# Attention passes: destination scores as float32r halves in one product, and work tables of 16-bit numbers

## The chip, the core and the metric

The kernel runs on one NeuronCore of a Trainium2 chip. The metric is the device time of one execution in microseconds. TensorE multiplies, VectorE (DVE), ScalarE (ACT) and GpSimd (POOL) do the rest, SyncE (SP) issues most DMAs and GpSimd the gathers. In the profile PE is TensorE's product and PEld its weight load; a name with q behind it (DVEq, ACTq, PEldq) is the sequencer of that engine, which loads registers, branches and waits.

## The reference

Four graph layers run one behind another on 3125 nodes with 256 features and 103125 edges, sorted by destination. Each starts with `h = relu(layernorm(x))` and adds its result to `x`: a typed attention layer (L0), a weighted sum over edges (L1), an edge MLP with a gate (L2), and a graph attention of two convolutions (L3). The change touches the two convolutions in earnest:

```python
h = (x @ W).reshape(N, HEADS, HEAD_DIM)            # 8 heads of 32
alpha_s = jnp.einsum('nhc,hc->nh', h, a_src)
alpha_d = jnp.einsum('nhc,hc->nh', h, a_dst)
e = alpha_s[src] + alpha_d[dst]
e = jnp.where(e > 0, e, NEG_SLOPE * e)
m = jax.ops.segment_max(e, dst, num_segments=N)
ex = jnp.exp(e - m[dst])
denom = jax.ops.segment_sum(ex, dst, num_segments=N)
alpha = ex / (denom[dst] + 1e-16)
out = jax.ops.segment_sum(h[src] * alpha[:, :, None], dst, num_segments=N)
```

## The kernel before

**Tiling.** Edges are taken in supertiles of 1024 (128 partitions x 8 slots); there are 102. Nodes lie in 25 blocks of 128. Since edges are sorted by destination, a supertile's destinations fall into one block, and into a second one for 24 of the 102 supertiles. What must be known of this is worked out on the chip by `prepare()` (lines 364 to 374) into two small tables on partition 0, `work` (line 163, blocks of 128 nodes) and `typed_work` (line 171, windows of 104 nodes for the typed pass). Row `s + 1` has four 32-bit numbers for supertile `s`: the numbers of the first extra block and of the one behind the last, the first block, and how many extra ones there are. An engine that needs them loads the row into registers: `work_of` (line 699) and `work_typed` (line 796).

**The passes.** In order: the typed pass (`typed_pass`), the weighted pass, the edge MLP pass, and then twice, for the layers of the graph attention: `gat_tables` (line 1979), `gat_pass` (line 2064) and `gat_normalise`. `gat_tables` computes, block by block, `h @ W` and the two scores of each node and head; it writes `h` with the source scores as rows of 264 numbers to a table in HBM and keeps the destination scores in `dst_alpha`, 25 x 8 numbers per partition (reduction at line 2044).

**One attention pass.** Three supertiles make a group (34 groups), two groups a turn of the hardware loop. Of a group with number q:

- GpSimd gathers the source rows (line 731), 8 gathers of 128 rows for each supertile, into one of six slots. A slot is free when the messages of the supertile five before the awaited count are made.
- SyncE loads destination numbers as rows (`dst_row`) and penalties for the scans.
- ACT makes of a row of destination numbers a one-hot matrix `hotrow` (lines 2285 and 2286: square of the difference to the node number, then relu(1 - square)), and `xhotrow` for an extra block.
- TensorE brings each edge the score of its destination (`expand`, `bring`, line 2370): for each of the 8 slots the one-hot matrix is the weight operand (128x128, float32) and the block's 8 destination scores are the moving one; the extra block is added into the same place of `psE`.
- VectorE adds the source scores from the gathered rows (line 2164) and takes the leaky relu (line 2166); TensorE turns the scores (line 2406), VectorE scans for the running maxima (lines 2244 and 2245), TensorE turns them back (line 2414).
- VectorE subtracts (`diff`, line 2253), ACT takes the exponential (line 2337), VectorE makes the messages (line 2233), and TensorE sums them by destination with a one-hot matrix (`scatter`, line 2385), and once more for an extra block. VectorE merges the sum into the node's values with the running maximum (`combine`, lines 2175 to 2186).

The order is written out by hand in the functions `group` of each engine. On TensorE a group is: scatter(0), the turned scores of the next group, scatter(1), scatter(2), the turning back for the next group, and then the three brings of the group after next:

```python
                        scatter(s + 2, 2, g % 2)
                        if next_scores:
                            turn_back(q + 1)
                        scatter_extra(s + 2, g % 2)
                        if next_rows:
                            for u in range(U):
                                expand(q + 2, u)
```

The next product in line is scatter(0) of the next group. On VectorE a group is: diff, messages(0), the scores of the next group, messages(1), combine(0), messages(2), the scans of the next group, combine(1), combine(2). A bring's product before the change:

```python
last = nc.tensor.matmul(group_view(psE)[:, j, u, :], onehots[:, j, :],
                        dst_alpha[:, ds(b, 1), :].squeeze(1), start=(fresh and j == 0),
                        stop=True, skip_group_check=True)
```

Of the kernel before, what the change touches and what calls it, by code (L numbers as in the profile page):

```python
# [19 lines left out]
F32 = mybir.dt.float32  # L20
BF16 = mybir.dt.bfloat16
I32 = mybir.dt.int32
ALU = mybir.AluOpType
# [3 lines left out]
P = 128  # L27
D = 256
SLOTS = 8
# [4 lines left out]
H3 = 8  # L34
DE = 64
U = 3
# [17 lines left out]
def ds(i, n):  # L54
    return bass.ds(i, n)
# [23 lines left out]
def gnn(nc, a, out, n_nodes, n_edges):  # L79
# [83 lines left out]
    work = sb(top, "work", [1, NS + 2 * U + 2, 4], I32)  # L163
# [7 lines left out]
    typed_work = sb(early, "typed_work", [1, NS + 2 * U + 2, 4], I32)  # L171
# [1807 lines left out]
    def gat_tables(layer, dst_alpha, elu_source):  # L1979


        with Stage(("h", "low", "low_exp", "elu", "hT_ps", "hT", "y", "rows", "alphas", "link_dve"), ("w_in", "r_out")) as st:
# [11 lines left out]
            with nc.Block() as block:  # L1994
# [28 lines left out]
                def _(dve):  # L2023
# [11 lines left out]
                    with dve.Fori(0, NB) as b:  # L2035
# [11 lines left out]
                        dve.wait_ge(S["alphas"], START + b + 1)  # L2047

# [15 lines left out]
    def gat_pass(layer, dst_alpha):  # L2064
# [6 lines left out]
        with Stage(("idx_staged", "scored", "hotrow", "expanded", "x_hotrow", "x_expanded", "to_scan_ps",  # L2071
# [8 lines left out]
            hotrow = st.sb("hotrow", [P, U, SLOTS, P])  # L2080
            xhotrow = st.sb("xhotrow", [P, SLOTS, P])
# [23 lines left out]
            lanes = psX[0:LANES, :]  # L2105

# [3 lines left out]
            with nc.Block() as block:  # L2110
# [42 lines left out]
                def _(dve):  # L2153
# [3 lines left out]
                    def edge_scores(i, g):  # L2157
                        q = 2 * i + g
                        for u in range(U):
                            slot_rows_in(dve, U * g + u, i)  # L2160
                        _, x1, _, _ = work_of(dve, U * q + U)
                        dve.wait_ge(S["expanded"], START + U * q + U)
                        dve.wait_ge(S["x_expanded"], START + x1)
                        link(v.tensor_tensor(et[:, :, :, :], group_view(psE),
                                             rows[:, U * g:U * g + U, :, D:GAT_W].rearrange("p u j h -> p j u h"), ALU.add))
                        v.scalar_tensor_tensor(et[:, :, :, :], et[:, :, :, :], 0.2, et[:, :, :, :], ALU.mult,
                                               ALU.max).then_inc(S["scored"], 1)
# [195 lines left out]
                def _(pe):  # L2363
                    def expand(q, u):
# [3 lines left out]
                        def bring(onehots, b, fresh):  # L2368
                            for j in range(SLOTS):
                                last = nc.tensor.matmul(group_view(psE)[:, j, u, :], onehots[:, j, :],  # L2370
                                                        dst_alpha[:, ds(b, 1), :].squeeze(1), start=(fresh and j == 0),
# [109 lines left out]
    with top:  # L2481
# [11 lines left out]
        dst_alpha = sb(top, "dst_alpha", [P, NB, H3])  # L2493
        weight = sb(middle, "weight", [P, NT + U * SLOTS])
# [13 lines left out]
        for layer in (1, 2):  # L2508
            gat_tables(layer, dst_alpha, layer == 2)
            gat_pass(layer, dst_alpha)  # L2510
# [52 lines left out]
```

## Time and profile before

| | |
|---|---|
| median of 3 runs | 8833.31 us |
| lowest, highest | 8825.69, 8842.84 us |
| span of the profiled execution | 8830.1 us |
| TensorE busy (products) | 6600.0 us, 75% |
| VectorE busy | 5164.4 us, 58% |
| GpSimd busy | 4060.3 us, 46% |
| ScalarE busy | 2234.7 us, 25% |
| mean granted TensorE clock | 0.819 of full speed |

The profiled execution is not one of the three timed ones. Its own time is known as its span, from the first to the last instruction, 8830.1 us, which is 3.2 us below the median. The span has five long stretches: the typed pass (about 600 to 2115 us), the weighted pass (2555 to 3690), the edge MLP pass (3860 to 5920) and the two attention passes (6095 to 7380 and 7505 to 8790). Between them lie short stages over the nodes. An engine that is busy for most of a stretch sets its length; where none is, the length comes from waits between the engines, which the timeline shows one by one.

### The profile page before, as it was taken

The page shows a single profiled execution, that of the slowest core. Times are in us where ns is not written, and L with a number is a line of the kernel's source. Part 1 is how long each engine was busy: PE and PEld are TensorE (multiplying, and loading weights), DVE is VectorE, ACT ScalarE, POOL GpSimd, SP SyncE. Part 2 cuts the span into 40 slices and gives each one's busy share as a digit, 9 for nine tenths or more (in the row PEclk, how much of TensorE's full clock was granted, in tenths as well). Part 3 has the DMA queues.
Part 4 walks back from the last instruction along what each step waited for, and adds up shares of the span by engine and source line. Part 5 has one row for each costly group of instructions (what it writes and reads, how often), then busy time and mean ns, then how long its engine had stood idle before and what let it go on. Part 6 is the DMA issues. An engine that isn't in the chain of part 4 may idle for free. (4 is left out here: it accounts for less than half of the span.)

```text
span 8830.1 us, 116392 instructions
## 1 busy us (share of the span) xinstructions
PE 6600.0 (75%) x27378; PEld 5018.6 (57%) x27379; DVE 5164.4 (58%) x9644; ACT 2234.7 (25%) x4857; POOL 4060.3 (46%) x4373
## 2 busy tenths in 40 slices
PE   4977777774736666679999999974788885787886
PEld 2546566563525444546666666653676673666665
DVE  3138888886243333246666666665666666566666
ACT  1222222221310000123333333332333331333332
POOL 0025555552037777124444444423666661666663
PEclk9988888886857777589999999986777776677777
DMA  2247767666013333133343344332444441544443
GB/s 92 99 144 212 214 208 213 207 209 151 4 57 105 105 105 105 29 108 115 115 124 114 116 121 116 117 83 85 135 139 135 131 140 37 149 133 135 136 135 90
DMA packets 440058, 1096.42 MB, mean 124 GB/s; under 512 B 102452, under 2 KB 177296, under 8 KB 439410
## 3 DMA queue, kind: packets, MB, share of 16 engines
q0 software_dynamic: 249344, 763.23, 30.9%
q1 hardware_dynamic: 190180, 328.60, 11.1%
q14 instruction: 507, 4.15, 0.2%
q8 instruction: 27, 0.44, 0.0%
HBM read 1009.55 MB, written 81.94 MB: 124 GB/s over the span
## 5 line engine op out<-in xcount | busy, mean ns | idle before, releaser
L731 POOL DMA_INDIRECT st_rows<-g_table,st_stage_idx x1632 | 1558.0, 955 | 873.4 <-issue 463.6
L824 POOL DMA_INDIRECT st_rows<-kv_table,st_stage_idx x832 | 806.2, 969 | 671.1 <-PE st_psM L1167 391.2
L2385 PE MATMUL st_psM<-st_msg,st_hot 128*128 128x273 f32 x3264 | 942.6, 449 | 128.0 <-DVE st_msg L2233 102.6
L677 POOL DMA_INDIRECT st_rows<-p_table,st_stage_idx x816 | 854.3, 1047 | 302.9 <-issue 220.3
L731 POOL DMA_INDIRECT st_rows<-h_table,st_stage_idx x816 | 777.0, 952 | 244.5 <-issue 234.8
L2385 PEld LDWEIGHTS st_psM<-st_msg,st_hot 128*128 128x128 f32 x3264 | 702.9, 221 | 321.5 <-DVE st_msg L2233 91.2
L1519 DVE TENSOR_TENSOR st_pre<-st_psP,st_rows 128x512 f32<-128x512 f32 x816 | 523.5, 682 | 531.5 <-PE st_psP L1610 392.6
L1616 PE MATMUL st_psC<-st_w,st_rT 128*128 128x256 f32 x3264 | 814.7, 392 | 0.0
L1616 PEld LDWEIGHTS st_psC<-st_w,st_rT 128*128 128x128 f32 x3264 | 587.3, 190 | 373.7 <-ACT st_rT L1577 212.3
L1426 PE MATMUL st_psM<-st_rows,st_hot 128*128 128x256 f32 x1632 | 512.3, 484 | 372.5 <-DMA st_rows<-h_table,st_stage_idx 190.4
L1426 PEld LDWEIGHTS st_psM<-st_rows,st_hot 128*128 128x128 f32 x1632 | 401.3, 251 | 480.7 <-issue 331.3
L1572 ACT ACTIVATE st_gate<-st_pre 128x256 f32<-128x256 f32 x816 | 340.4, 417 | 1276.2 <-DVE st_pre L1519 1276.2
L2370 PE MATMUL st_psE<-dst_alpha,st_hotrow 128*128 x3264 | 589.7, 323 | 66.5 <-issue 34.2
L2370 PEld LDWEIGHTS st_psE<-dst_alpha,st_hotrow 128*128 128x128 f32 x3264 | 585.6, 281 | 72.8 <-issue 70.8
L1149 PE MATMUL st_psE<-st_q_rows,st_hotrow 104*128 104x256 f32 x1664 | 513.5, 477 | 39.6 <-ACT st_hotrow L1076 18.5
L673 POOL COPY st_stage_idx<-src_idx 128x8 int32 x102 | 19.3, 189 | 1117.1 <-DVE st_pre L1519 850.5
L2233 DVE TENSOR_TENSOR st_msg<-st_rows,st_psU 128x2048 f32<-128x2048 f32 x204 | 465.4, 2281 | 111.1 <-ACT st_psU L2337 111.1
L1610 PE MATMUL st_psP<-st_wb,st_eaT 64*128 64x512 f32 x1632 | 461.6, 642 | 53.4 <-DVE st_pre L1519 47.8
L1149 PEld LDWEIGHTS st_psE<-st_q_rows,st_hotrow 104*128 104x128 f32 x1664 | 404.0, 249 | 128.7 <-issue 33.9
L1167 PE MATMUL st_psM<-st_rows,st_hot 128*128 128x262 f32 x1632 | 376.7, 389 | 51.3 <-DVE st_rows L1035 51.1
L2385 PE MATMUL st_psZ<-st_msg,st_xhot 128*128 128x273 f32 x768 | 253.9, 498 | 202.9 <-DVE st_xhot L715 202.9
L1361 DVE TENSOR_TENSOR node_values<-node_values,st_psM 128x256 f32 x228 | 94.8, 416 | 510.1 <-PE st_psM L1426 385.3
(394 smaller groups left out, 11250.1 us busy)
## 6 DMA issues: line engine op xcount, KB each, us to landing
st_dst_row<-in_dst_row SPq DMA_DIRECT2D x310, 512.0 KB, 5.7
kv_table<-st_rows_out SPq DMA_DIRECT2D x25, 1560.0 KB, 5.7
st_ea<-in_ea SPq DMA_DIRECT2D x103, 256.0 KB, 3.8
st_rows<-g_table,st_stage_idx POOLq DMA_INDIRECT x1632, 2.8
st_pens<-pen_table SPq DMA_DIRECT2D x208, 72.0 KB
st_rows<-kv_table,st_stage_idx POOLq DMA_INDIRECT x832, 4.5
st_rows<-h_table,st_stage_idx POOLq DMA_INDIRECT x816, 2.7
st_rows<-p_table,st_stage_idx POOLq DMA_INDIRECT x816, 3.7
```

The costliest lines, as they stand in the source:

```text
L677: pool.indirect_dma_start(out=rows[:, u * SLOTS + j, :], out_offset=None, in_=table, in_offset=bass.IndirectOffsetOnAxis(ap=stage_idx[:, u ...
L731: pool.indirect_dma_start(out=rows[:, slot, j, :], out_offset=None, in_=table, in_offset=bass.IndirectOffsetOnAxis(ap=stage_idx[:, g, u * ...
L824: pool.indirect_dma_start(out=rows[:, slot, j, :], out_offset=None, in_=kv_table, in_offset=bass.IndirectOffsetOnAxis(ap=stage_idx[:, g, u ...
L1149: last = nc.tensor.matmul(psE[h][:, j * D:(j + 1) * D], onehots[0:NQ, h * HALF + j, :], queries, start=(fresh and j % 2 == 0), stop=True, ...
L1167: last = nc.tensor.matmul(out[:, 0:SUM_W], onehots[:, j, :], rows[:, slot, j, D:D + SUM_W], start=(j == 0), stop=(j == SLOTS - 1))
L1426: last = nc.tensor.matmul(out[:, 0:D], onehots[:, j, :], rows[:, slot, j, :], start=(j == 0), stop=(j == SLOTS - 1))
L1519: v.tensor_tensor(pre[:, j % DEEP, :], psP[y][:, :], rows[:, u * SLOTS + j, :], ALU.add).then_inc(S["pre"], 1)
L1610: nc.tensor.matmul(psP[y][:, :], eaT[lo:lo + DE, u, k, :], wb[lo:lo + DE, :], start=True, stop=True).then_inc(S["pre_ps"], 1)
L1616: last = nc.tensor.matmul(psC[y][:, 0:D], rT[:, (2 * k + y) % DEEP, c, :], w2[:, c, :], start=(c == 0), stop=(c == 1))
L2233: v.tensor_tensor(msg[:, n, :, 0:GAT_W].rearrange("p j (h c) -> p j h c", h=H3)[:, :, :, 0:HW3 - 1], rows[:, slot, :, 0:D].rearrange("p j ...
L2370: last = nc.tensor.matmul(group_view(psE)[:, j, u, :], onehots[:, j, :], dst_alpha[:, ds(b, 1), :].squeeze(1), start=(fresh and j == 0), s ...
L2385: last = nc.tensor.matmul(out[:, 0:MSG_W], onehots[:, j, :], msg[:, n, j, :], start=(j == 0), stop=(j == SLOTS - 1))
```

## The change

The destination scores are kept a second time as `dst_split`, in float32r, a float32 with a shortened mantissa: a high half (the score converted) and a low half (what the conversion left off). The one-hot matrices are float32r too. One product per slot brings both halves, 16 columns instead of 8, into `psE`; VectorE adds the high halves to the source scores and then the low ones. The two work tables hold unsigned 16-bit numbers instead of 32-bit ones; the functions that read them are unchanged.

```diff
-    work = sb(top, "work", [1, NS + 2 * U + 2, 4], I32)
+    work = sb(top, "work", [1, NS + 2 * U + 2, 4], U16)
...
-    typed_work = sb(early, "typed_work", [1, NS + 2 * U + 2, 4], I32)
+    typed_work = sb(early, "typed_work", [1, NS + 2 * U + 2, 4], U16)
...
-    def gat_tables(layer, dst_alpha, elu_source):
+    def gat_tables(layer, dst_alpha, dst_split, elu_source):
...
                         last.then_inc(S["alphas"], 1)
                         dve.wait_ge(S["alphas"], START + b + 1)
+                    link.turn()
+                    link(v.tensor_copy(dst_split[:, :, 0, :], dst_alpha[:, :, :]))
+                    link(v.tensor_tensor(dst_split[:, :, 1, :], dst_alpha[:, :, :], dst_split[:, :, 0, :].bitcast(F32), ALU.subtract))
...
-            hotrow = st.sb("hotrow", [P, U, SLOTS, P])
-            xhotrow = st.sb("xhotrow", [P, SLOTS, P])
+            hotrow = st.sb("hotrow", [P, U, SLOTS, P], F32R)
+            xhotrow = st.sb("xhotrow", [P, SLOTS, P], F32R)
...
+            def split_view(n):
+                return psE[:, 0:SLOTS * U * 2 * H3].rearrange("p (j u n h) -> p j u n h", j=SLOTS, u=U, n=2)[:, :, :, n, :]
+
...
-                        link(v.tensor_tensor(et[:, :, :, :], group_view(psE),
+                        link(v.tensor_tensor(et[:, :, :, :], split_view(0),
                                              rows[:, U * g:U * g + U, :, D:GAT_W].rearrange("p u j h -> p j u h"), ALU.add))
+                        link(v.tensor_tensor(et[:, :, :, :], split_view(1), et[:, :, :, :], ALU.add))
...
-                                last = nc.tensor.matmul(group_view(psE)[:, j, u, :], onehots[:, j, :],
-                                                        dst_alpha[:, ds(b, 1), :].squeeze(1), start=(fresh and j == 0),
+                                at = (j * U + u) * 2 * H3
+                                last = nc.tensor.matmul(psE[:, at:at + 2 * H3], onehots[:, j, :],
+                                                        dst_split[:, ds(b, 1), :, :].rearrange("p b n h -> p (b n h)"), start=(fresh and j == 0),
                                                         stop=True, skip_group_check=True)
...
+        dst_split = sb(top, "dst_split", [P, NB, 2, H3], F32R)
```

## Rows read from the trace of the kernel before

**Rows 1.** Busy time by stretch: us, PE, PEld, DVE, ACT, POOL, PEclk, DMA share, GB/s

```profile
600.00:2115.00 1515.00, 1098.48 (x4322) 902.33 (x4321) 1310.61 (x1772) 351.19 (x483) 812.06 (x880) 0.81 0.70 209
2555.00:3690.00 1135.00, 713.97 (x2230) 558.20 (x2230) 362.79 (x1244) 22.09 (x48) 785.04 (x851) 0.74 0.34 95
3860.00:5920.00 2060.00, 1919.67 (x8956) 1346.93 (x8956) 1353.23 (x2831) 713.47 (x1842) 868.76 (x913) 0.98 0.40 117
6095.00:7380.00 1285.00, 1017.18 (x4576) 861.62 (x4576) 793.42 (x1310) 415.13 (x918) 785.14 (x848) 0.75 0.45 131
```

**Rows 2.** Costliest groups: xcount | busy us, mean ns | idle before them, releasers

```profile
L731 POOL DMA_INDIRECT st_rows<-g_table,st_stage_idx x1632 | 1558.0, 955 | 873.4 <-issue 463.6
...
L2385 PE MATMUL st_psM<-st_msg,st_hot 128*128 128x273 f32 x3264 | 942.6, 449 | 128.0 <-DVE st_msg L2233 102.6
...
L2370 PE MATMUL st_psE<-dst_alpha,st_hotrow 128*128 x3264 | 589.7, 323 | 66.5 <-issue 34.2
...
L2370 PE MATMUL st_psE<-dst_alpha,st_xhotrow 128*128 x768 | 169.8, 359 | 74.0 <-ACT st_xhotrow L2286 73.7 <-issue 0.2
```

**Rows 3.** Waits from 6095 to 8790 us: us in total, times, longest

```profile
POOL st_rows L731 <- DVE st_msg L2233: 400.4, 95, 12.2
...
DVE st_et L2164 <- DMA st_rows<-g_table,st_stage_idx: 173.0, 19, 22.5
...
DVE st_et L2164 <- PE st_psE L2370: 133.0, 32, 7.8
...
PE st_psE L2370 <- ACT st_xhotrow L2286: 73.7, 27, 3.1
```

**Rows 4.** Timeline of TensorE, four groups: start us, us, merged instructions, idle before

```profile
6465.13 10.18 PE L2370 MATMUL st_psE<-dst_alpha,st_hotrow 128*128 x48 [1.12 <-issue]
...
6478.57 5.85 PE L2385 MATMUL st_psM<-st_msg,st_hot 128*128 128x273 f32 x16
...
6505.89 6.90 PE L2370 MATMUL st_psE<-dst_alpha,st_hotrow 128*128 x48
6515.89 5.98 PE L2385 MATMUL st_psM<-st_msg,st_hot 128*128 128x273 f32 x16 [3.10 <-DVE st_msg L2233]
...
6548.03 3.58 PE L2370 MATMUL st_psE<-dst_alpha,st_xhotrow 128*128 x16 [1.88 <-ACT st_xhotrow L2286]
6551.46 3.56 PE L2370 MATMUL st_psE<-dst_alpha,st_hotrow 128*128 x16
6554.87 6.94 PE L2385 MATMUL st_psM<-st_msg,st_hot 128*128 128x273 f32 x16
...
6587.78 5.87 PE L2385 MATMUL st_psM<-st_msg,st_hot 128*128 128x273 f32 x16 [1.45 <-DVE st_msg L2233]
```

**Rows 5.** Timeline of VectorE in the same groups

```profile
6472.64 2.29 DVE L2233 TENSOR_TENSOR st_msg<-st_rows,st_psU 128x2048 f32<-128x2048 f32 x1 [2.07 <-ACT st_psU L2337]
6480.09 0.36 DVE L2164 TENSOR_TENSOR st_et<-st_psE,st_rows 128x192 f32<-128x192 f32 x1 [5.16 <-DMA st_rows<-g_table,st_stage_idx]
...
6484.46 0.16 DVE L2175 TENSOR_SCALAR st_absent<-st_psM 128x1 f32<-128x1 f32 x1 [1.29 <-PE st_psM L2385]
...
6548.11 2.29 DVE L2233 TENSOR_TENSOR st_msg<-st_rows,st_psU 128x2048 f32<-128x2048 f32 x1 [2.02 <-ACT st_psU L2337]
6555.15 0.36 DVE L2164 TENSOR_TENSOR st_et<-st_psE,st_rows 128x192 f32<-128x192 f32 x1 [4.75 <-PE st_psE L2370]
```

**Rows 6.** Two lines of TensorE, weight loads: duration ns min/median/max, first and last start

```profile
L1616 PEld LDWEIGHTS st_psC<-st_w,st_rT x3264: 186/190/337, 3875.7 to 5913.4; 128*128 128x128 f32 x192
...
L1624 PEld LDWEIGHTS st_psR<-ident,st_pre x1632: 139/140/144, 3878.5 to 5914.1; 128*128 128x128 f32 x182
```

**Rows 7.** VectorE's loads in the typed pass (line 797), and idle time before `hot` there

```profile
L797 DVEq TENSOR_LOAD <-typed_work x308: 337/344/754, 592.9 to 2106.4; - x154
...
DVE st_hot L715 <- issue: 98.0, 51, 2.4
```

**Rows 8.** The leaky relu at line 2166: duration ns min/median/max

```profile
L2166 DVE SCALAR_TENSOR_TENSOR st_et<-st_et x68: 357/358/407, 6125.4 to 8742.8; 128x192 f32<-128x192 f32 x68
```

More of the change, by code:

```diff
@@ L20 @@
 F32 = mybir.dt.float32
+F32R = mybir.dt.float32r
 BF16 = mybir.dt.bfloat16
 I32 = mybir.dt.int32
+U16 = mybir.dt.uint16
 ALU = mybir.AluOpType
@@ L2062, in _, with gat_pass @@
                         last.then_inc(S["y"], 1)
-    def gat_pass(layer, dst_alpha):
+    def gat_pass(layer, dst_split):
         with Stage(("idx_staged", "scored", "hotrow", "expanded", "x_hotrow", "x_expanded", "to_scan_ps",
@@ L2508, in gnn @@
         for layer in (1, 2):
-            gat_tables(layer, dst_alpha, layer == 2)
-            gat_pass(layer, dst_alpha)
+            gat_tables(layer, dst_alpha, dst_split, layer == 2)
+            gat_pass(layer, dst_split)
             group_passes[0] += 1
```

## The prediction

> **What bounds the kernel now.** I read the passes one by one first. In the typed pass VectorE is busy 1310.6 of 1515 us, in the weighted pass GpSimd issues gathers all the time, in the edge MLP pass TensorE is busy 1919.7 of 2060 us at a clock of 0.98 [rows 1]. The work tables are read in all of them. The reader should see that only the two attention passes (1285 us each) have no engine near its limit: TensorE 1017 us, VectorE 793 us, GpSimd 785 us plus its issue gaps. They are bound by a ring of waits.
>
> The ring, per group of three supertiles: TensorE turns the scanned maxima back, brings the destination scores of the group after next (line 2370), and only then can start scatter(0), the first of the group's three message sums (line 2385). VectorE in that time makes `diff` and the first messages, and then waits for psE and the gathered rows (line 2164). GpSimd needs 24 x (955 + 300) ns = 30.1 us for a group's gathers [rows 2]; two groups of the timeline take 6548.11 - 6472.64 = 75.5 us, 37.7 each [rows 5]. So the gathers are not the bound: GpSimd waited 400.4 us for messages to free its slots [rows 3].
>
> **The change, part by part. First the size of the product.** A bring is eight products. Today each is two records (204 brings, 3264 records; 48 extra ones, 768), 589.7 + 169.8 = 759.5 us busy [rows 2]. Sixteen records take 3.58 us at the low clock, 0.22 us each; three brings that began at the high one took 6.90 us, 0.144 each [rows 4]. The moving side is only 8 columns, so the pace is that of the weight loads. A float32 load takes 190 ns and a load for a transpose, which is one record per product over the same 128 columns, 140 ns [rows 6]; latency included, that is one pass of columns less. I take a float32r product as one record with a one-pass load: half the records, half the time of each, a bring of 0.9 us instead of 3.58. The 16 moving columns stay under the load. Upper end: half the records at the old pace, 1.8 us. Lower end: 8 x 0.06, 0.5 us. TensorE sheds 570 us by the middle value, 380 by the upper end.
>
> **What of that is on the path.** I follow four groups in the timelines [rows 4, 5].
> - Group one: the brings ran until scatter(0) began at 6478.57, though its messages were done at 6474.93. But VectorE then stood until 6480.09 for gathered rows, not for psE. What is won is its later wait for scatter(0), 1.3 us.
> - Group two: scatter(0) at 6515.89 had waited 3.10 us for messages. The three brings were covered. Won: 0.
> - Group three: TensorE waited for ACT's extra one-hot until 6548.03, then ran two brings to 6555.0. With 0.9 us each they end at 6549.8, ahead of the messages (6550.40). VectorE's 4.75 us wait for psE goes, scatter(0) starts at 6550.5 instead of 6554.87: 4.4 us won.
> - Group four: scatter(0) waited 1.45 us for messages. Won: 0.
>
> That is 5.7 us in four groups; the pattern of extra blocks repeats about so, and there are 68 groups: 17 x 5.7 = 97 us. The other count is the total of VectorE's waits for psE, 133.0 us in 32 groups [rows 3]. Four groups are a small sample, so I take the middle of the two, 115 us. Lower end 54: bring of 1.8 us, group three wins 3.2, group one nothing. Upper end 133 + 17 x 1.3 = 155.
> What is late next, where the brings go: the messages themselves (groups two and four), ACT's extra one-hot row (TensorE waited 73.7 us for it [rows 3], and still will), and gathered rows (173.0 us [rows 3]).
>
> **The added operation.** VectorE adds the low halves: one more 128x192 operation per group, 358 ns [rows 8], 0.39 us start to start with its link, ahead of `scored`, for which the turned scores on TensorE wait. In groups two to four VectorE stands after it for scatter(0) anyway, so it is covered there; behind it in group one are messages(1) and GpSimd's slot. 17 x 0.39 = +7 us; without cover 68 x 0.39 = +27.
> **Tables.** Two more operations over 200 elements after the loop of each layer, 4 x 0.39 = 1.5 us, while the last rows of the table are on their way to HBM: I cost them at 0 to 1.5, take 1. ACT writes the one-hot rows as float32r, same count and shape: 0; the bound, 5% of 1148 ns, would be hidden while ACT, busy 415 of 1285 us [rows 1], stands idle, except ahead of the extra bring.
>
> **The work tables.** Each read of a table row is already one load of four numbers; on VectorE it takes 344 ns [rows 7]. Narrower numbers leave the count of loads alone. The trace has no load of another width. One end: it becomes as cheap as a register operation, near 60 ns, -0.28 each; other end: narrow reads cost as much more, +0.28. Exposed are those ahead of which VectorE has nothing queued: in the typed pass the idle time before `hot` is 98.0 us in 51 groups [rows 7], 1.9 us each, two loads of it, and one more ahead of the scores: 3 x 51 = 153. In the attention passes, with the engines waiting on one another, I count 1.5 per group, 100. In the weighted and the MLP pass GpSimd and TensorE cover them. Half the bytes may save a little and are unlikely to save most: I take -0.06, 250 x -0.06 = -15 us; ends -70 and +70.
> The Trainium skill (DMA: Bandwidth & Descriptors, "Latency and other measured facts") gives `tensor_load` a floor of about 600 ns. The trace does not agree (344 ns). If there is a floor all the same, at this trace's own value, then the width saves nothing and the sum would be 15 us less.
>
> **The sum.** -115 + 7 + 1 - 15 = -122 us against the profiled span of 8830.1 us: 8708. The median of the runs is 8833.3, 3 us above that execution, so 8711, and I say 8710. What a measurement of this kernel can tell from no change is 0.2%, 18 us.
>
> **The rivals.**
> - *More than that.* VectorE's waits for psE all go, waits for scatter(0) with them, and the loads really get short: 155 + 70 = 225 less, 8605. For it: the 400.4 us that GpSimd stands waiting, so nothing stops it until a group takes 30.1 us. Against: groups two and four win nothing. Chance 0.17, from 8570 to 8640.
> - *Mostly hidden.* The bring stays at 1.8 us, the messages, the extra one-hot and the gathered rows take over, the added operation is on the path everywhere: -54 + 27 + 0 = -27, 8806. For it: two of four groups. Chance 0.14, 8770 to 8815.
> - *It does not do what it says.* A float32r product with so few moving columns is still run as two records with two-pass loads. Then nothing is saved and 7 to 27 us are added: 8840 to 8860, or with cheaper loads no change. Chance 0.07.
> - *Slower: the clock.* The sums are priced by TensorE's clock. 204 of them take 942.6 us, 4.62 each [rows 2]; one that began at the low level took 6.94 [rows 4]. With the brings short, TensorE stands idle for longer ahead of each sum, and more of them could begin or stay at 1.2 GHz. If the mean rises half-way to 6.94, to 5.8: 204 x 1.2 = +240 us, less the 122: 8950. It decides from a rise of 0.6 us per sum (122/204). Against: scatter(0) begins at the low level today as well (5.85, 5.98, 6.94 and 5.87 us in the four groups [rows 4]), because the brings do not keep the clock up, so there is little left to lose. Chance 0.07.
> The Trainium skill (TensorE: Matmul & The Clock Gate, "What's actually happening") says that throttled is the default and activity releases it. By that rule a TensorE with less work is the slower one per product, and this rival would come in; the trace agrees that idle stretches and small products go with the low clock, and speaks for no loss only by the four rows just named.
>
> **How the numbers follow.** Likeliest, 0.55: the ring loosens by what the brings delayed, 8640 to 8770, told as 8710. The range reaches over it and most of its two neighbours, from 8600 (both upper ends) to 8800 (lower end of the product, little from the loads). Outside are the clock, no effect and the tails. Faster by over 0.2%: 0.55 + 0.17 + 0.14 = 0.86; within 0.2%: most of the third rival, 0.05; slower: the clock and the rest, 0.09.
>
> **What the profile of the changed kernel would show.** At line 2370 (shifted) 1632 + 384 records instead of 3264 + 768, busy under 250 us, loads near 140 ns at the high clock. VectorE's wait for psE at the first score addition under 30 us instead of 133.0. GpSimd's wait for messages down by about 100 from 400.4. Scatter(0) directly behind its messages in all groups without an extra block, mean of the sums still 4.4 to 4.9 us. TENSOR_LOAD on VectorE between 0.25 and 0.344 us, and the typed pass shorter by up to 10 us; the weighted and the MLP pass unchanged. It is wrong if the records do not halve (third rival), if sums get longer than 5.2 us (fourth), or if the waits for gathered rows and for ACT's one-hot grow by what the brings gave up (second).

## The result and the profile after

The change makes the kernel slower. In paired runs before took 8832.07 us (median of 4) and after 9124.14 us (9118.15 to 9131.29): ratio 1.0332, 95% interval 1.0319 to 1.0345, 292 us more. The profiled execution of after has a span of 9128.0 us, 297.9 more than that of before.

Where the time came in is read first, by the first and the last gather of each pass. Kernel before, the gathers of one table each (duration ns min/median/max, first to last start):

```profile
L824 POOL DMA_INDIRECT st_rows<-kv_table,st_stage_idx x832: 941/947/1745, 593.7 to 2079.8; - x167
...
L731 POOL DMA_INDIRECT st_rows<-h_table,st_stage_idx x816: 942/947/1067, 2558.1 to 3585.7; - x164
...
L677 POOL DMA_INDIRECT st_rows<-p_table,st_stage_idx x816: 942/947/1912, 3854.2 to 5879.2; - x164
...
L731 POOL DMA_INDIRECT st_rows<-g_table,st_stage_idx x1632: 940/947/1198, 6092.7 to 8727.7; - x182
```

Kernel after, the same rows:

```profile
L826 POOL DMA_INDIRECT st_rows<-kv_table,st_stage_idx x832: 940/946/1917, 604.9 to 2255.3; - x167
...
L733 POOL DMA_INDIRECT st_rows<-h_table,st_stage_idx x816: 942/946/1066, 2732.8 to 3758.6; - x164
...
L679 POOL DMA_INDIRECT st_rows<-p_table,st_stage_idx x816: 941/947/1912, 4025.6 to 6109.6; - x164
...
L733 POOL DMA_INDIRECT st_rows<-g_table,st_stage_idx x1632: 940/946/1218, 6323.8 to 9031.1; - x182
```

The typed pass is 164 us longer (1650.4 against 1486.1), the weighted pass nearly the same (1025.8, 1027.6), the edge MLP pass 59 us longer (2084.0, 2025.0), the attention passes 72 (2707.3, 2635.0). The three that grew account for 295 of the 297.9 us. The float32r product is in the attention passes alone, so in the typed and the edge MLP pass only the tables can be at work. The loads of the tables in after (against VectorE's 344 ns in [rows 7]):

```profile
L799 DVEq TENSOR_LOAD <-typed_work x308: 941/949/1615, 604.1 to 2280.8; - x154
...
L703 PEldq TENSOR_LOAD <-work x612: 981/987/1009, 2731.9 to 9080.9; - x153
L703 ACTq TENSOR_LOAD <-work x612: 879/887/937, 6322.7 to 9081.7; - x153
...
L703 DVEq TENSOR_LOAD <-work x476: 942/948/970, 2740.0 to 9083.5; - x159
```

A load of four 16-bit numbers takes 949 ns on VectorE, 0.60 us more than one of four 32-bit numbers. Their count is the same (308). VectorE's idle time ahead of its work in the typed pass shows it; after, with before's row for `hot` in [rows 7] (98.0 us in 51) and before's other row at line 950 below it:

```profile
DVE st_hot L717 <- issue: 234.8, 101, 4.6
DVE st_rows L952 <- issue: 63.9, 51, 1.3
```

```profile
DVE st_rows L950 <- issue: 33.0, 51, 0.7
```

"Issue" is time in which the engine waited for nothing that the profile shows but its own sequencer: 136.8 + 30.9 = 168 us more, about the typed pass's 164. The product itself did what it says; TensorE's groups in the attention passes of after, answering to [rows 2]:

```profile
L2395 PE MATMUL st_psM<-st_msg,st_hot 128*128 128x273 f32 x3264 | 953.0, 453 | 284.5 <-DVE st_msg L2242 183.4 <-issue 101.0
L2380 PE MATMUL st_psE<-dst_split,st_hotrow 128*128 x1632 | 320.3, 330 | 129.1 <-issue 96.0 <-ACT st_hotrow L2295 33.1
...
L2380 PE MATMUL st_psE<-dst_split,st_xhotrow 128*128 x384 | 89.8, 363 | 185.7 <-ACT st_xhotrow L2295 185.7
```

The records have halved (1632 + 384) and the busy time with them, 759.5 to 410.1 us (320.3 + 89.8). But each still takes 330 ns, as before (323).

### The profile page after: what moved, and what is told of

It reads as the page before. It is cut to its first block and busy times, and to the rows that moved or that the text cites. A ratio compares the mean times of both kernels' runs of the same rounds, so it can differ in the third digit from the quotient of the medians.

```text
span 9128.0 us, 112436 instructions
## 1 busy us (share of the span) xinstructions
PE 6326.0 (69%) x25362; PEld 4709.1 (52%) x25363; DVE 5189.8 (57%) x9716; ACT 2255.5 (25%) x4857; POOL 4075.6 (45%) x4373
## 5 line engine op out<-in xcount | busy, mean ns | idle before, releaser
L733 POOL DMA_INDIRECT st_rows<-g_table,st_stage_idx x1632 | 1561.3, 957 | 950.0 <-DVE st_msg L2242 476.4
L2395 PE MATMUL st_psM<-st_msg,st_hot 128*128 128x273 f32 x3264 | 953.0, 453 | 284.5 <-DVE st_msg L2242 183.4
L1618 PEld LDWEIGHTS st_psC<-st_w,st_rT 128*128 128x128 f32 x3264 | 587.2, 190 | 373.7 <-ACT st_rT L1579 212.3
L1428 PEld LDWEIGHTS st_psM<-st_rows,st_hot 128*128 128x128 f32 x1632 | 393.1, 246 | 483.7 <-issue 328.2
L1151 PE MATMUL st_psE<-st_q_rows,st_hotrow 104*128 104x256 f32 x1664 | 551.0, 504 | 85.0 <-issue 60.9
L1151 PEld LDWEIGHTS st_psE<-st_q_rows,st_hotrow 104*128 104x128 f32 x1664 | 430.2, 265 | 185.5 <-issue 79.1
L2380 PE MATMUL st_psE<-dst_split,st_hotrow 128*128 x1632 | 320.3, 330 | 129.1 <-issue 96.0
L1169 PEld LDWEIGHTS st_psM<-st_rows,st_hot 128*128 128x128 f32 x1632 | 315.1, 196 | 151.7 <-issue 100.4
L2380 PEld LDWEIGHTS st_psE<-dst_split,st_hotrow 128*128 128x128 f32 x1632 | 309.7, 287 | 139.0 <-issue 137.1
```

What stands on the lines that cost most here:

```text
L733: pool.indirect_dma_start(out=rows[:, slot, j, :], out_offset=None, in_=table, in_offset=bass.IndirectOffsetOnAxis(ap=stage_idx[:, g, u * ...
L1151: last = nc.tensor.matmul(psE[h][:, j * D:(j + 1) * D], onehots[0:NQ, h * HALF + j, :], queries, start=(fresh and j % 2 == 0), stop=True, ...
L1169: last = nc.tensor.matmul(out[:, 0:SUM_W], onehots[:, j, :], rows[:, slot, j, D:D + SUM_W], start=(j == 0), stop=(j == SLOTS - 1))
L1428: last = nc.tensor.matmul(out[:, 0:D], onehots[:, j, :], rows[:, slot, j, :], start=(j == 0), stop=(j == SLOTS - 1))
L1618: last = nc.tensor.matmul(psC[y][:, 0:D], rT[:, (2 * k + y) % DEEP, c, :], w2[:, c, :], start=(c == 0), stop=(c == 1))
L2380: last = nc.tensor.matmul(psE[:, at:at + 2 * H3], onehots[:, j, :], dst_split[:, ds(b, 1), :, :].rearrange("p b n h -> p (b n h)"), start= ...
```

## The experiments

Times are compared by their ratio to the kernel before, run beside each group of experiments on the same chip: its median was 8831.20 us beside e1 to e4, 8828.58 beside e9 to e12 and 8837.26 beside e13 to e16. e5 to e8 ran on a chip on which the kernel before itself takes 10409.62 us. Every variant with a 32-bit table also masks the two loaded numbers that waits are made against. e1 is the kernel before with the mask and one more operation on a semaphore in the typed pass's stores by SyncE (`hold(sp, held)`, in all of these variants), and they are read against it; e3, with no 32-bit table, has no mask and is read against the kernel before. Pass lengths and waits come from one profiled execution of each kernel.

**e1: the mask.**

```diff
+    def masked(eng, values, top):
+        x0, x1, low, more = values
+        x0, x1 = (nc.s_assert_within(eng.snap(x & 0xFFFF), 0, top, skip_runtime_bounds_check_because=BOUNDED) for x in (x0, x1))
+        return x0, x1, low, more
...
-        return values
+        return masked(eng, values, NS * NB)
```

> The kernel before with 32-bit tables, whose two waited-on numbers are also cut to 16 bits in registers (two or so register operations of about 40 ns per load): the base for the float32r part alone. Both theories: loads 340 ns on VectorE as before, 8832 plus 15 to 45 us, so 8850 to 8880.

Measured: 8818.12 us, ratio 0.9986 (0.9976 to 0.9995), not the 8850 to 8880 that I had expected.

**e2: the product alone**, the changed kernel with `I32` in both tables, and the mask.

> The same base plus the whole float32r part, tables of 32 bits. Theory A (the 16-bit loads cost all of the loss and the float32r part gains as in the ring of waits): 100 to 140 us below the base of this call, so about 8740; periods of the attention groups near 35.3 us, VectorE's wait for psE almost gone. Theory B (the shorter products lower the clock or lengthen the sums, and share in the loss): not below the base, 8860 to 8950, mean of the sums over 4.8 us.

Measured: 8782.53 us, 0.9947 (0.9931 to 0.9964). The product gains, as theory A has it, but 36 us against e1 and not 100 to 140.

**e3: the tables alone**, the kernel before with `U16` in both.

> The kernel before with both tables of 16-bit numbers and nothing else. Theory A: loads about 949 ns on VectorE as in the changed kernel; typed pass +164 us, MLP pass +59 us, attention passes +160 us, together 9215. Theory B: the attention passes lose much less by the loads, 9060 to 9120.

Measured: 9168.05 us, 1.0386 (1.0369 to 1.0403); typed pass 1647.7 us, as in after. It lies between the two theories: the typed pass is 162 us longer than before and the edge MLP pass 55, as expected, and the attention passes 110, not 160. So the loss is the tables', +337 us against before, and the product takes some 44 us off it (9168.05 - 9124.14, of two pairs of runs).

**e4: what a load costs.** A stage of loads of each kind, twice, from tiles in SBUF, is added after `prepare`; its own time is not of interest.

```diff
+                    use(dve, [load(w32[0:1, 0:4], engines=[dve.engine], **KW) for _ in range(2)])
+                    use(dve, [load(w32[0:1, 1:5], engines=[dve.engine], **KW) for _ in range(2)])
+                    use(dve, [load(w16[0:1, 0:1], engines=[dve.engine], **KW) for _ in range(2)])
```

> The 16-bit kernel with a small stage behind the preparation in which VectorE and TensorE load 1, 2, 3 or 4 numbers of 32, 16 or 8 bits. Theory A1 (each narrow number is a read of its own, four 32-bit ones are one): 32 bits 1 to 4 numbers all 340 ns on VectorE; 16 bits about 340 for one number and 200 more for each further one: 340, 545, 745, 949. Theory A2 (narrow reads are slow as such, or each load of several takes a slower route): 16 bits near 949 ns whatever the number.

VectorE's loads: L2510 to L2514 are 2, 3, 4, 4 from the second element on, and 8 of 32 bits; L2515 to L2518 are 1, 2, 3 and 4 of 16 bits; L2519 is 4 of 8 bits:

```profile
L2510 DVEq TENSOR_LOAD <-st_w x2: 523/528/532, 84.0 to 84.6; - x2
...
L2511 DVEq TENSOR_LOAD <-st_w x2: 743/748/753, 85.7 to 86.4; - x2
...
L2512 DVEq TENSOR_LOAD <-st_w x2: 348/353/358, 87.7 to 88.1; - x2
...
L2513 DVEq TENSOR_LOAD <-st_w x2: 961/963/965, 89.1 to 90.1; - x2
...
L2514 DVEq TENSOR_LOAD <-st_w x2: 597/598/599, 91.7 to 92.4; - x2
...
L2515 DVEq TENSOR_LOAD <-st_w x2: 289/292/295, 93.7 to 94.1; - x2
...
L2516 DVEq TENSOR_LOAD <-st_w x2: 503/508/513, 94.7 to 95.3; - x2
...
L2517 DVEq TENSOR_LOAD <-st_w x2: 722/724/725, 96.3 to 97.1; - x2
...
L2518 DVEq TENSOR_LOAD <-st_w x2: 941/946/952, 98.3 to 99.3; - x2
...
L2519 DVEq TENSOR_LOAD <-st_w x2: 961/964/968, 101.3 to 102.3; - x2
```

One 16-bit number takes 292 ns and each further one some 218 (292, 508, 724, 946); two and three of 32 bits (528, 748) and four of 8 bits (964) take about as much as that many of 16 bits. Four of 32 bits from the start of the tile are the exception: 353 ns, less than two (528), and eight take 598. The same four from the next element on take 963. So theory A1 holds for the 16-bit numbers and for four of 32 bits; it was wrong for two and three of 32 bits, which it had at 340. The times fit one read of 16 bytes in place of four. That what counts is a start on a 16-byte boundary is inferred: the start of the tile and a start 4 bytes behind it were tried, 8 bytes were not.

**e9: is it the width or the single read?** 32-bit tables, four bytes off the boundary.

```diff
-    work = sb(top, "work", [1, NS + 2 * U + 2, 4], I32)
+    work = sb(top, "work", [1, 4 * (NS + 2 * U + 2) + 4], I32)[:, 1:4 * (NS + 2 * U + 2) + 1].rearrange("p (n k) -> p n k", k=4)
```

> The kernel before with its 32-bit tables (and the mask of the first experiment), but both tables begin four bytes later, so that no row of four numbers starts on a 16-byte boundary. Nothing else differs: same width, same number of loads, same order. Theory (what the change costs is the duration of the load alone, four reads of about 215 ns in place of one, whatever the reason that the four don't come in one): TENSOR_LOAD on VectorE goes from 344 ns to 940 to 965, and the time to a ratio of 1.036 to 1.040 against the kernel before, as with the 16-bit tables alone (1.0386), 1.0386 x 0.9986 = 1.037 with the mask's share. Rival (it is the width: 16-bit numbers are unpacked or converted, a 32-bit row is read in one whatever its address): loads stay at 344 ns, ratio 0.9986 as for the masked kernel.

Measured: 9194.99 us, 1.0413 (1.0395 to 1.0430), a little over what was expected. The load:

```profile
L802 DVEq TENSOR_LOAD <-typed_work x308: 958/967/1549, 599.1 to 2297.0; - x154
```

So it is not the width that costs: the same 32-bit table loads as slowly, and loses as much, when it is moved by four bytes. What both have in common is the time of the load, 949 and 967 ns, and e4's times say that the four numbers then no longer come in one read.

**e13, e14, e15: whose loads stand on the path?** Every table is there twice, on the boundary and off it; one engine alone reads the slow copy.

```diff
+    SLOW = (nc.vector.engine,)
...
-            work[0:1, ds(row, 1), :].squeeze(1), engines=[eng.engine], min_val=0, max_val=NS * NB,
+            (work_slow if eng.engine in SLOW else work)[0:1, ds(row, 1), :].squeeze(1), engines=[eng.engine], min_val=0, max_val=NS * NB,
```

> The kernel before (with the mask), where every table is there twice, on a 16-byte boundary and four bytes behind one, and VectorE alone reads the second: its 690 loads take 960 us/1000 each in place of 344, those of the other engines are as before. With all engines slow the time was up 377 us from the masked kernel: 173 in the typed pass, 86 in the edge MLP pass, 112 in the attention passes. Theory (a load counts in full on the engine that bounds its pass, because that engine's queue runs in order and its linked operations leave nothing queued): VectorE bounds the typed pass, 308 loads x 0.62 = 190, so nearly all of the 173 stands here, nothing of the weighted pass, little of the MLP pass (TensorE's), and in the ring of the attention passes two loads a group, at most 2 x 68 x 2 x 0.62 = 168, some 60 to 110: ratio 1.025 to 1.032. Rival (the loads of all engines count alike, by the waits of each on the other): its share of the loads, about a third, 125 us, ratio 1.013.

> The same with TensorE's loads alone slow (332 to 1000 ns, 0.67 us more). Theory: the edge MLP pass, where TensorE is busy over 0.9 of the time, has one load a supertile, 102 x 0.67 = 68 us at most; nothing in the typed and the weighted pass; three loads a group in the attention passes, of which those ahead of a bring are hidden and the one ahead of scatter(0) may not be, 0 to 50. Ratio 1.005 to 1.012. Rival (all alike): 1.013 with at least 50 us of it in the typed pass.

> The same with ACT's loads alone slow (308 to 900 ns, 0.59 us more), 612 of them in the attention passes, 206 in the typed pass. Theory: ACT is busy a third of the time, its one-hot rows are made ahead; only the load ahead of the extra one-hot row, for which TensorE waits 84 us in all, comes through: 48 x 0.59 = 28 us, ratio 0.999 to 1.003. Rival (all alike): 1.013.

Measured: VectorE 9135.80 us, 1.0341 (1.0323 to 1.0358), above the expected range; TensorE 8867.57 us, 1.0036 (1.0022 to 1.0051), below it; ACT 8871.10 us, 1.0037 (1.0024 to 1.0049), a little above it. In all three the rival that every engine's loads count alike is out (1.013). Pass lengths by first and last gather, in us more than in e1 (1496.2, 1026.3, 2032.1 and 2597.8):

| slow loads | typed | weighted | edge MLP | attention |
|---|---|---|---|---|
| all (e9) | 173 | 2 | 86 | 112 |
| VectorE (e13) | 171 | 1 | 74 | 52 |
| TensorE (e14) | 3 | 2 | 1 | 53 |
| ACT (e15) | 4 | 2 | 1 | 46 |

The three add up to 0.0456 of the time (each against e1's 0.9986), all together to 0.0427. By pass the three come to 178 us in the typed pass (173 with all slow at once) and 76 in the edge MLP pass (86), but to 151 in the attention passes where all at once bring 112: there the delays of one engine cover part of another's. (The profiled execution of e14 was the slowest of its five, 16 us above their median, so its 53 may be too much by up to that. SyncE's loads, slow in e9 too, were not tried alone.) In the typed pass nothing but VectorE's loads counts: 306 of them, six a group, by 0.62 us are 190, and 171 arrive. My expectation for the edge MLP pass was wrong: TensorE is the busiest there [rows 1], yet its own loads cost 1 us, and VectorE's 102, 102 x 0.62 = 63 us, arrive in full (74 us). Its queue stands between TensorE's products: `pre` waits for psP, and TensorE for `pre`. That second wait grows, in e1 and in e13:

```profile
PE st_psP L1616 <- DVE st_pre L1525: 48.5, 93, 0.7
```

```profile
PE st_psP L1622 <- DVE st_pre L1531: 117.2, 192, 0.8
```

That TensorE's own loads cost nothing there because its sequencer runs ahead of its products is argued, not shown. In the attention ring no engine's loads are hidden, and none arrive whole: alone, they cost 0.19 us for each of VectorE's 272, 0.13 for each of TensorE's 408 (six a group, where I had written three) and 0.08 for each of ACT's 612.

**e16: the typed table alone as 16-bit numbers.**

> The typed pass's table alone as 16-bit numbers (with the mask on the other), on the chip of these runs. On the slower chip it cost 0.45% against the masked kernel's -0.14%. In the changed kernel the typed pass is 164 us longer: 164/8830 = 1.86%, so 1.0172 with the mask, if the passes add up; near 1.003 if the typed pass gives its loss back later, or if the loss comes from something else in the changed kernel.

Measured: 8980.06 us, 1.0161 (1.0144 to 1.0178). The typed pass is 151 us longer than in e1 (1647.3 against 1496.2), and the loss stays to the end. The same kernel on the slow chip (e8) lost much less:

> The kernel before with only the typed pass's table in 16 bits (the other one 32 bits, its waited-on numbers cut to 16 bits in registers). Theory A: the typed pass grows by 150 us as in the kernel with both, the other passes stay: 8818 + 150 = 8970. If the loads of the other passes also counted there, or the typed pass's growth came from elsewhere, the pass would grow by less than 130.

Measured there: 10438.92 us, 1.0031 (1.0016 to 1.0045), with loads as long (948 ns). The typed pass is 1732.8 us there, only 18 more than with 32-bit tables on the same chip (1715.3 in e5): that pass was already 219 us longer than in e1, and VectorE has other waits there. Which of them covers the loads was not followed.

**e10, e12, e11: the product again, doubled, and in bf16.** The doubled one issues each product a second time, into columns that nobody reads. The other replaces float32r by bf16 in the one-hot rows and in the halves.

```diff
+                                last = nc.tensor.matmul(psE[:, 384:384 + 2 * H3], onehots[:, j, :],
+                                                        dst_split[:, ds(b, 1), :, :].rearrange("p b n h -> p (b n h)"), start=False,
+                                                        stop=True, skip_group_check=True)
```

```diff
-            hotrow = st.sb("hotrow", [P, U, SLOTS, P], F32R)
+            hotrow = st.sb("hotrow", [P, U, SLOTS, P], BF16)
...
-        dst_split = sb(top, "dst_split", [P, NB, 2, H3], F32R)
+        dst_split = sb(top, "dst_split", [P, NB, 2, H3], BF16)
```

> The float32r product and its second addition alone, with 32-bit tables and the mask, again, beside the next two on one chip. If the chip is like the one of the first runs: ratio 0.9947 as before, 0.993 to 0.9965. On the slower chip the doubled product gave 0.9959, so this must be at or under it: 0.990 to 0.996.

> The float32r kernel with each of a bring's products issued twice (the second into unused columns of the same bank): the records of a bring are back at 16, the second addition stays. If the shorter bring is what the float32r kernel gains: 0.9947 goes back to 0.9986 (the mask alone) plus the second addition, 0.9986 to 1.000, that is 35 to 45 us above the kernel of the run before last. If the gain has another source (fewer columns to read for the weights, the shape of the PSUM tile), the time stays within 10 us of it.

> As the kernel with the float32r product, but the one-hot rows and the two halves are bf16: same count of products and records, same 16 columns, the second addition kept. Theory A (what is left of a bring is set by the pace of the weight load, 0.23 us a record, and the ring gets what it gives up): a bring falls below 1.2 us from 1.62, 0.4 us or more x 48 extra and some of the 204 others on the path, 10 to 40 us less than the float32r kernel, ratio 0.989 to 0.994. Theory B (the brings are already hidden behind the messages, the extra one-hot of ACT and the rows): within 10 us of the float32r kernel, unless ACT writes bf16 rows faster; its waits move by as much. ACT's one-hot row for the extra block is the row that tells: 1148 ns before; if it stays and TensorE's wait for it (171.5 us) stays, B.

Measured: float32r 8784.54 us, 0.9948 (0.9931 to 0.9964); doubled 8822.42 us, 0.9993 (0.9984 to 1.0003); bf16 8753.33 us, 0.9910 (0.9894 to 0.9927). The weight loads of a bring, in before, in e10 and in e11:

```profile
L2370 PEld LDWEIGHTS st_psE<-dst_alpha,st_hotrow x3264: 186/333/338, 6098.6 to 8741.9; 128*128 128x128 f32 x192
```

```profile
L2386 PEld LDWEIGHTS st_psE<-dst_split,st_hotrow x1632: 186/333/338, 6125.7 to 8703.8; 128*128 128x128 f32 x182
```

```profile
L2386 PEld LDWEIGHTS st_psE<-dst_split,st_hotrow x1632: 95/99/118, 6122.3 to 8667.7; 128*128 128x128 bf16 x182
```

float32r halves the number of records and leaves each weight load as long as float32's; bf16 loads in 99 ns. With the records doubled again the gain is gone (38 us), and VectorE's wait for psE is back (213.0 us in e1, 35.6 in e10, 205.3 in e12), so the gain came from the shorter bring. And bf16 wins 31 us more, so what is left of a bring still counts. ACT writes its row for the extra block as fast in bf16 (1147 ns in e10 and in e11), so that is not the source, and TensorE's wait for that row grows from 171.5 to 242.3 us as the brings shrink.

The busy time of a bring in e11, 0.37 us, is not its pace. Three of them in a row:

```profile
6481.35 0.36 PE L2386 MATMUL st_psE<-dst_split,st_hotrow 128*128 x8 [1.02 <-issue]
6482.35 0.35 PE L2386 MATMUL st_psE<-dst_split,st_hotrow 128*128 x8 [0.65 <-issue]
6483.40 0.35 PE L2386 MATMUL st_psE<-dst_split,st_hotrow 128*128 x8 [0.69 <-issue]
```

From start to start it is 1.04 us in the median, where TensorE waits for its own sequencer between them; in e10 it is 1.71 and in before 3.41. Where the rest stays is read from TensorE's groups of e1, e10 and e11:

```profile
L2391 PE MATMUL st_psM<-st_msg,st_hot 128*128 128x273 f32 x3264 | 953.8, 453 | 94.6 <-DVE st_msg L2239 94.4
...
L2391 PE MATMUL st_psZ<-st_msg,st_xhot 128*128 128x273 f32 x768 | 245.7, 485 | 188.3 <-DVE st_xhot L720 188.3
L2376 PE MATMUL st_psE<-dst_alpha,st_xhotrow 128*128 x768 | 171.3, 361 | 84.5 <-ACT st_xhotrow L2292 84.4
```

```profile
L2401 PE MATMUL st_psM<-st_msg,st_hot 128*128 128x273 f32 x3264 | 962.0, 456 | 196.2 <-DVE st_msg L2248 196.2
L2386 PE MATMUL st_psE<-dst_split,st_hotrow 128*128 x1632 | 301.0, 321 | 66.9 <-ACT st_hotrow L2301 34.2 <-issue 32.6
L2401 PE MATMUL st_psZ<-st_msg,st_xhot 128*128 128x273 f32 x768 | 287.8, 550 | 255.3 <-DVE st_xhot L722 255.3
L2386 PE MATMUL st_psE<-dst_split,st_xhotrow 128*128 x384 | 89.7, 363 | 171.5 <-ACT st_xhotrow L2301 171.5
```

```profile
L2401 PE MATMUL st_psM<-st_msg,st_hot 128*128 128x273 f32 x3264 | 961.8, 456 | 284.6 <-DVE st_msg L2248 284.6
L2401 PE MATMUL st_psZ<-st_msg,st_xhot 128*128 128x273 f32 x768 | 278.2, 535 | 265.1 <-DVE st_xhot L722 265.1
...
L2386 PE MATMUL st_psE<-dst_split,st_hotrow 128*128 x1632 | 74.5, 173 | 147.6 <-issue 108.2 <-ACT st_hotrow L2301 38.7
...
L2386 PE MATMUL st_psE<-dst_split,st_xhotrow 128*128 x384 | 18.2, 176 | 242.9 <-ACT st_xhotrow L2301 242.3 <-issue 0.6
```

From e1 to e10 the brings shed 368 us (759.0 to 390.7). TensorE's waits take 256 of them: for messages +102, for the extra block's `xhot` of VectorE +67, for its one-hot row of ACT +87. The extra sums take 42 more (245.7 to 287.8), the others 8. The attention passes got 22 us shorter (2597.8 to 2575.7). The 42 us are the clock, as the duration of a record tells (ns min/median/max; in e1, e10 and e12):

```profile
L2391 PE MATMUL st_psZ<-st_msg,st_xhot x768: 391/394/819, 6223.2 to 8761.1; 128*128 128x273 f32 x192
```

```profile
L2401 PE MATMUL st_psZ<-st_msg,st_xhot x768: 391/662/819, 6232.7 to 8740.8; 128*128 128x273 f32 x192
```

```profile
L2404 PE MATMUL st_psZ<-st_msg,st_xhot x768: 391/394/819, 6225.6 to 8764.4; 128*128 128x273 f32 x192
```

More than half of these records are long in e10, and with the brings doubled they are as in e1 again: with less work ahead of it, an extra sum more often runs at the low level. The wait ahead of it is as in e1 again, too (190.2 us), so whether the missing brings or the longer wait lowers the clock is not told apart.

**e5, e6, e7 on the slow chip**: the doubled product, the high halves alone (the low halves and the second addition left out), bf16.

> The float32r kernel with 32-bit tables (8783 us) in which each bring's product is issued twice, the second time into columns of psE that nobody reads: a bring is as long again as before the change, 16 records. Theory C (the shorter brings did reach the ring, but little of them is on it): about 0.3 to 0.6 us per group and the added VectorE operation, 8800 to 8840. Theory D (the brings' length is on the path in full, 2.6 us per group at scatter(0), and something else of the change gives it back): 8783 + 68 x 2 = 8920 or more.

> The float32r kernel with 32-bit tables, with only the high halves brought (8 columns) and without the second addition on VectorE; the low halves of the destination scores are left out. If the added VectorE operation stood on the path in all 68 groups: 27 us less, 8756. Theory C: in a part of the groups, 5 to 15 us less, 8768 to 8778. Records of the products stay at 0.23 us each at the low clock whether 8 or 16 columns move, since the weight load sets their pace.

> The float32r kernel with 32-bit tables, with the one-hot rows and both halves in bfloat16 instead (a destination score keeps about 16 bits of mantissa). It tells what sets the pace of a float32r record: if its load takes two passes because the number has four bytes, a 2-byte load is shorter, the bring under 1.0 us instead of 1.55 to 1.87. Theory C: the time is then nearly the same, 8765 to 8785, since the brings are no longer awaited. Theory D: 68 x 1 us less or more, below 8730.

Measured: 0.9959 (0.9942 to 0.9976), 0.9933 (0.9908 to 0.9958) and 0.9901 (0.9872 to 0.9930). The doubled product is faster than the kernel before there, which it is not on the other chip (e12, 0.9993); why is open, and neither the masked kernel nor the float32r product as it is ran on this one. bf16 with both halves and both additions is no slower than float32r with one of each. What the second addition costs alone was not separated.

**The best version** is e11, 32-bit tables on their 16-byte boundary and bf16 halves: 8753.33 us, 0.9% under before and 4.1% under the change (0.9910/1.0332 = 0.959).

## Why the prediction was wrong

I gave 8710 us, 8600 to 8800, and slower a chance of 0.09; it is 9124. The step that failed is the **work tables** term: "One end: it becomes as cheap as a register operation, near 60 ns, -0.28 each; other end: narrow reads cost as much more, +0.28 ... ends -70 and +70", -15 taken. It failed twice.

- *Size.* +0.60 us a load (344 to 949 ns) where I had bounded it at +0.28. I said that the trace has no load of another width and then bounded the price symmetrically about the one there is. But 344 ns for four numbers was the special case, not the middle. "Half the bytes may save a little" was the wrong unit: by e4's times what counts is the number of reads.
- *Count.* The tables alone cost 337 us (e3 against before), 337/0.60 = 560 loads' worth, not 250. In the typed pass I took three a group from the idle time before `hot`; all six of VectorE's count (171 us of 190). The edge MLP pass, 59 us in after, I had taken as covered by TensorE. It is VectorE's queue that isn't covered. In the attention passes I had 100 loads in full; there no engine's arrive in full, but TensorE's and ACT's, slow alone, cost about as much as VectorE's.

With the measured size my own count gives 250 x 0.60 = +150 and the sum 8710 + 15 + 150 = 8875, the right sign. By terms: the tables were -15 and are +337; the product with its added operations was -107 and is about -34 (e10 against e1). The rival on the slower side, the **clock**, did not come in as told: the mean of the 204 sums in after is 953.0/204 = 4.67 us against 4.62. It shows in small in the 48 extra sums, which begin after a wait: 245.7/48 = 5.1 us in e1 and 287.8/48 = 6.0 in e10, 42 us lost there, because more of their records run at the low level (median 394 and 662 ns). The mean granted clock of the stretch hides this: 0.74 in e10, 0.75 in the first of these passes before [rows 1].

The sign of being wrong that the prediction gave for this term would have told at once: VectorE's load was to take 0.25 to 0.344 us and the typed pass to be up to 10 us shorter; they are 0.949 us and 164 us longer. GpSimd's wait for messages was to fall by about 100 from 400.4 us; in after it is 476.4. VectorE's wait for psE was to fall under 30 us and did, to 16.9.

**The size of the product.** "Half the records" held. "Half the time of each" did not: a bring in e10 is 390.7/252 = 1.55 us, near my upper end (1.8), not 0.9. The bring of before was mis-sized as well: 3.58 us is one at the low level, over all 252 it is 759.5/252 = 3.01, so brings of 0.9 would have shed 533 us and not 570. The row I took the short load from [rows 6] is a transpose's; it didn't say how a float32r product loads. The profile was to show under 250 us busy and loads near 140 ns at the high clock; it shows 410.1 us, and loads of 186 ns at best.

**What of that is on the path.** For 1.8 us I had 54 us; e10 against e1 gives 0.0038 of 8829, 34 us, with the second addition in it, of which 7 were forecast: the ring as I followed it held roughly, a little under its lower end (54 - 7 = 47). For a shorter bring it held less well: 0.9 us was to give 115, less 7 for the addition, and e11, whose brings start 1.04 us apart, gives 67 (0.0076). The second rival, **mostly hidden**, describes this best: the extra one-hot row, the messages and the gathered rows took over. VectorE's wait for psE, 213.0 us in e1, is down to 35.6 in e10; its wait for gathered rows rose from 75.9 to 199.9 us in e10, TensorE's for the extra row from 84.4 to 171.5. GpSimd waited 344.0 us for messages in place of 370.6. Without the tables (and with the mask) the change comes out at 0.995 (e2, e10), faster as forecast, yet only just inside the range.

**Two figures of the Trainium skill.** The load of four numbers in before, 344 ns [rows 7], and the median of e4's loads of one 16-bit number, 292 ns, are under the floor of about 600 that the prediction cited from the Trainium skill (DMA: Bandwidth & Descriptors), so that floor is not this instruction's from SBUF. Another page of the Trainium skill comes nearer to the case, Runtime: NRT & Kernel Launch, section "Instruction fetch mechanics": it gives a load of registers about 200 ns per register, even in bulk, where it speaks of loads from HBM and not from SBUF. e4 comes near to it for narrow numbers and for those that start one element on (218 ns for each further one), and not for four 32-bit ones from the start of the tile, which together take 353. Four registers at 200 ns would be 800 by that page, an estimate; beside it the 344 ns of [rows 7] would have shown that the load of before was a cheap case with more to lose than to gain. I had not looked at it.

## What to carry to other kernels

A price that the trace shows once is not the middle of its range: ask first whether the row is an exception that the edit takes away. In this kernel tables for registers are best kept as groups of four 32-bit words from the start of their tile: packing them narrower, or shifting them by four bytes, costs 0.6 us a load. In the typed and the edge MLP pass VectorE's loads bring nearly all of that, in the second although TensorE is the busiest there; those of TensorE and ACT bring next to nothing in these two. To shorten a product with few moving columns look at its weight load: float32r removed one of two records and left the load as long, bf16 shortened the load as well.

## What was not expected of the hardware

- Four 32-bit numbers from the start of a tile load faster (353 ns) than two (528) or three (748).
- float32r weights load as long as float32's (186 ns at best, 333 at the median) though a product is one record; bf16's take 95 to 118 ns.
- The mask adds register operations behind every load and the kernel got 0.14% faster for it (e1): its attention passes are 37 us shorter (2597.8 against 2635.0), the typed and the edge MLP pass 10 and 7 longer. Why was not tried; the added semaphore operation is in it as well.
- On one chip the kernel before took 18% more (10409.62 against 8831.20 us), and e5 to e8 about as much. In e5 there GpSimd waited for messages three times as long as in e12, the same kernel, elsewhere (373.7 us):

```profile
POOL st_rows L738 <- DVE st_msg L2248: 1193.7, 110, 26.1
```

GpSimd's wait is not where it begins, as far as the trace tells: ahead of its message sums TensorE in e5 is idle 196.1 us with nothing that it waits for, in e12 hardly at all, and in e5 there are gaps of about 2 us between single products of one sum (such as those that start at 7428.44 and 7430.54 us). The cause is open.
